# Ordering one-hots in batches of eight columns, a 52 + 28 + 80 scatter, and a three-pass mish

## Time and profile before

| | us |
|---|---|
| median of 3 runs | 2331.24 |
| lowest and highest | 2323.88, 2334.01 |
| the profiled execution's own time | 2325.94 |
| its span | 2324.2 |

### The profile page before, as it was taken

The page is one execution under the profiler, slowest core; times in us unless marked ns, Lnnn a source line. Parts: engine busy times, 40 slices in busy tenths (PEclk is TensorE's granted clock), DMA queues, the critical chain, the costliest instruction groups (busy, mean ns, idle before and its releaser), DMA issues. The chain is left out here.

```text
span 2324.2 us, 36961 instructions
## 1 busy us (share of the span) xinstructions
PE 2038.3 (88%) x11455; PEld 1106.1 (48%) x11455; DVE 1774.2 (76%) x3095; ACT 1456.0 (63%) x2429; POOL 1291.8 (56%) x1065
## 2 busy tenths in 40 slices
PE   0787688789988949999999987999999999999865
PEld 0433577546655624444444453455555554555422
DVE  8999899853333348888888853999999999999723
ACT  1999777421122225555555534999999999999822
POOL 0576677518810034444444204788888888888530
PEclk9999999989989969999999999999999999999988
DMA  2410100112143244333333304232222222222000
GB/s 114 165 27 14 55 0 0 59 32 78 41 123 98 83 139 142 93 100 99 95 93 95 71 16 134 87 92 76 77 74 76 75 74 74 77 70 78 10 0 22
DMA packets 81562, 170.33 MB, mean 73 GB/s; under 512 B 17378, under 2 KB 43221, under 8 KB 80449
## 3 DMA queue, kind: packets, MB, share of 16 engines
q0 software_dynamic: 35840, 98.88, 15.6%
q1 hardware_dynamic: 45624, 70.25, 9.1%
HBM read 144.93 MB, written 23.98 MB: 73 GB/s over the span
## 5 line engine op out<-in xcount | busy, mean ns | idle before, releaser
L884 PE MATMUL e_two_ps<-w,e_first 128*128 128x512 bf16 x1408 | 419.8, 380 | 0.1
L1629 ACT ACTIVATE u_msg<-u_t,slot_record 128x128 f32<-128x128 f32 x704 | 223.3, 390 | 98.0 <-DVE u_t L1685 97.9
L643 POOL DMA_INDIRECT sorted_records<-edge_record,slot_row x160 | 209.9, 1312 | 123.6 <-issue 57.8
L884 PE MATMUL e_two_ps<-w,e_first_low 128*128 128x512 bf16 x704 | 267.3, 380 | 0.0
L1813 POOL TENSOR_TENSOR e_first_low<-e_first 128x1024 bf16<-128x1024 f32 x88 | 250.1, 2842 | 21.9 <-DVE e_first L2004 21.9
L1818 POOL TENSOR_TENSOR e_msg_low<-e_act 128x1024 bf16<-128x1024 f32 x88 | 225.6, 2563 | 55.9 <-DVE e_act L2016 54.7
L1547 POOL DMA_INDIRECT u_got<-up_table,u_idx x176 | 185.0, 1051 | 76.8 <-issue 43.7
L2309 POOL DMA_INDIRECT e_got<-src_table,e_idx x176 | 186.6, 1060 | 70.5 <-issue 35.5
L884 PEld LDWEIGHTS e_two_ps<-w,e_first 128*128 128x128 bf16 x1408 | 134.4, 98 | 148.6 <-issue 2.2
L685 PE MATMUL pairs_ps<-cell_high,src_hot 128*128 128x144 bf16 x1180 | 153.0, 227 | 44.5 <-POOL cell_rest L709 22.4
L1593 PE MATMUL u_sum_ps<-u_msg,u_hot 128*125 128x512 f32 x352 | 185.1, 608 | 7.5 <-ACT u_msg L1629 7.5
(11 more groups left out here) (366 smaller groups left out, 5140.6 us busy)
## 6 DMA issues: line engine op xcount, KB each, us to landing
conv_w<-in_L_gnn_basis_dram SPq DMA_DIRECT2D x8, 1024.0 KB
sorted_records<-pairs SPq DMA_DIRECT2D x5, 1408.0 KB, 10.9
edge_record<-in_edge_floats_dram SPq DMA_DIRECT2D x2, 3125.0 KB
later_w<-in_L_gnn_W_dram SPq DMA_DIRECT2D x6, 1024.0 KB
attr_parts<-h SPq DMA_DIRECT2D x22, 256.0 KB, 2.1
e_attrT<-attr_parts SPq DMA_DIRECT2D x44, 128.0 KB
e_dst_all<-dst_row SPq DMA_DIRECT2D x44, 125.0 KB
pairs<-in_edge_floats_dram SPq DMA_DIRECT2D x1, 3125.0 KB
```

Of the source, the lines that this page charges most:

```text
L643: pg.nc.gpsimd.indirect_dma_start(out=pg.sorted, out_offset=bass.IndirectOffsetOnAxis(ap=pg.slot_row[:, j:j + 1], axis=0), in_=pg.edge_rec ...
L884: last = nc.tensor.matmul(out, lhsT, rhs, start=(n == 0), stop=(n == len(pairs) - 1))
L1629: last = nc.scalar.activation(msg[:, k, at * MUL:(at + 1) * MUL], t12[:, k % 2, of], ACT.Copy, scale=pg.record[:, bass.ds(t, 1), Y + m])
```

## The change: what it does

1. **Ordering.** The loop goes over 20 batches of eight columns. For each, DVE runs four TENSOR_TENSOR operations on 16-bit operands: the lane one-hots (1024 elements per partition), the tile one-hots (1888), the key parts (2048) and all three weight parts (3072). Arrays are laid out with the eight columns innermost, so each matmul reads both of its operands with a step of eight elements (16 bytes). There are two buffers rather than four. PE's products stay 40 per batch. A constant `iota_eights` of 1888 elements is added. ACT makes no weight parts; it clears `pairs` in 16 pieces of 690 floats. POOL clears 12,800 floats ahead of its scatters and the last 4,960 (which hold one-hots in the loop) after `placed`. The semaphore `decoded` goes.
2. **Scatter.** 52 columns in `order_pairs`, 5 + 23 in `layer0` around the bias additions, 80 in the first convolution as before. The late records come in two DMAs: 52 columns in `build_pairs`, 28 at the end of SP's work in `layer0`, once all 80 have landed; ACT's last work in `layer0` waits for the second and names their ends.
3. **Mish.** Exp; DVE makes `(e + 2) * e` where it clamped; Ln with a scale and a bias; Exp. The Square passes go.
4. **Destination rows.** PE reads the table of destination rows directly, at an index that its own queue loads in each `first_layer`; the copy L1974 and DVE's register load go.
5. **One-hots of the edge MLP.** `e_hotT` and `e_hot` are made by one TENSOR_TENSOR each; POOL makes `lane_rows` once.
6. `place_edges`: one more ACT copy, and six copies of the ends rather than four.

The second copies of functions that differ only in a number (mish 2, for one) are left out of the diff.

```diff
+FIRST = 52
+BATCH = 8
...
+LOG_SCALE = 0.75 * 2.0 ** -64
+LOG_BIAS = 2.0 * LOG_SCALE
+SHARE_BIAS = float(np.log(2.0) + np.log(LOG_SCALE))
...
+    pg.iota_eights = pg.hT[:, :, :].rearrange("p f n -> p (f n)")[:, PT:PT + PT * BATCH // 2].bitcast(BF16)\
+        .rearrange("p (t j) -> p t j", j=BATCH)
...
+            nc.gpsimd.iota(pg.iota_eights[:, :, :], [[1, PT], [0, BATCH]], base=0, channel_multiplier=0,
+                           allow_small_or_imprecise_dtypes=True)
...
+            act.wait_ge(sem["weight_left"], 2)
+            nc.scalar.copy(weight_16[:, 2, :], pg.weight_part[:, 2, :])
+            for ends, at in ((pg.edge_record[0:EP, 0:EARLY, SRC:SRC + 2], slice(0, EARLY)),
+                             (pg.late_ends, slice(EARLY, EARLY + FIRST)), (pg.last_ends, slice(EARLY + FIRST, EC))):
...
+        lane_hot = pg.sb("pair_lane_hot", [EP, 2, P, BATCH], BF16, ctx)
+        BATCHES, WAITED = EC // BATCH, 4
+        CLEARED = (EC - EARLY) * RECORD + EC * BUCKETS
+        pairs = pg.pairs[:, :, :, :].rearrange("p s n d -> p (s n d)")
+        HOTS = pairs.shape[1] - (3 * P + PT) * BATCH
+        weight_hot = pairs[0:EP, HOTS:HOTS + 3 * P * BATCH].bitcast(BF16).rearrange("p (s c l j) -> p s c l j", s=2, c=3, l=P)
+        tile_hot = pairs[0:EP, HOTS + 3 * P * BATCH:].bitcast(BF16).rearrange("p (s t j) -> p s t j", s=2, j=BATCH)
...
+        key_hot = room[0:EP, 0:2 * P * BATCH].bitcast(FP16).rearrange("p (s c l j) -> p s c l j", s=2, c=2, l=P)
...
             nc.gpsimd.memset(zero[:, :], 0.0).then_inc(zeroed, 1)
+            nc.gpsimd.memset(pairs[:, 0:CLEARED], 0.0)
             pool.wait_ge(pg.emptied, 16 * 5)
-            scatter_records(pg, range(0, EARLY))
-            pool.wait_ge(decoded, 1)
-            pairs = pg.pairs[:, :, :, :].rearrange("p s n d -> p (s n d)")
-            size = pairs.shape[1] // 4
-            for n in range(1, 4):
-                nc.gpsimd.memset(pairs[:, n * size:(n + 1) * size], 0.0)
+            scatter_records(pg, range(0, FIRST))
+            pool.wait_ge(placed, 1)
+            nc.gpsimd.memset(pairs[:, HOTS:], 0.0)
...
+            for i in range(BATCHES):
+                s = i % 2
+                pe.wait_ge(keys_hot, i + 1)
+                for j in range(BATCH):
                     for c in range(2):
-                        nc.tensor.matmul(column(c), key_hot[:, s, c, :], tile_hot[:, s, :], start=False, stop=False)
-                    pe.wait_ge(weights_hot, STRIDE * i + n + 1)
+                        nc.tensor.matmul(column(c), key_hot[:, s, c, :, j], tile_hot[:, s, :, j], start=False, stop=False)
+                pe.wait_ge(weights_hot, i + 1)
+                for j in range(BATCH):
                     for c in range(3):
-                        last = nc.tensor.matmul(column(2 + c), weight_hot[:, s, c, :], tile_hot[:, s, :],
+                        last = nc.tensor.matmul(column(2 + c), weight_hot[:, s, c, :, j], tile_hot[:, s, :, j],
                                                 start=False, stop=False)
-                    last.then_inc(free, 1)
+                last.then_inc(free, 1)
...
+            size = (HOTS - CLEARED) // (BATCHES - WAITED)
+            for i in range(BATCHES):
+                act.wait_ge(lanes_hot, i + 1)
+                if i >= WAITED:
+                    act.wait_ge(pg.emptied, 16 * 5)
+                    at = CLEARED + (i - WAITED) * size
+                    to = pairs[:, at:at + size]
+                    nc.scalar.activation(to, pg.ones[:, 0:1].broadcast_to(list(to.shape)), ACT.Copy, scale=0.0)
...
+            def over(x, size):
+                return x.rearrange("p (a j) -> p a j", a=1).broadcast_to([EP, size, BATCH])
+            def parts(x):
+                return x.rearrange("p c (a j) -> p c a j", a=1).broadcast_to([EP, x.shape[1], P, BATCH])
+            def lanes(s, size):
+                return lane_hot[:, s, :, :].rearrange("p (a l) j -> p a l j", a=1).broadcast_to([EP, size, P, BATCH])
+            for i in range(BATCHES):
+                s = i % 2
+                at = slice(BATCH * i, BATCH * (i + 1))
+                dve.wait_ge(free, i + 1)
+                nc.vector.tensor_tensor(lane_hot[:, s, :, :], pg.iota_eights[0:EP, 0:P, :], over(pg.pair_lane[:, at], P),
+                                        ALU.is_equal).then_inc(lanes_hot, 1)
+                nc.vector.tensor_tensor(tile_hot[:, s, :, :], pg.iota_eights[0:EP, :, :], over(pg.pair_tile[:, at], PT),
+                                        ALU.is_equal)
+                dve.wait_ge(lanes_hot, i + 1)
+                nc.vector.tensor_tensor(key_hot[:, s, :, :, :], lanes(s, 2), parts(pg.key_part[:, :, at]),
+                                        ALU.mult).then_inc(keys_hot, 1)
+                nc.vector.tensor_tensor(weight_hot[:, s, :, :, :], lanes(s, 3), parts(pg.weight_16[:, :, at]),
+                                        ALU.mult).then_inc(weights_hot, 1)
...
-            dve.sem_inc(decoded, 1)
...
+def late_records(pg, sp, begin, end):
+    sp.dma_start(pg.edge_record[0:EP, begin:end, :],
+                 pg.inp["edge_floats"].rearrange("(p j) r -> p j r", j=EC)[:, EARLY + begin:EARLY + end, :])\
+        .then_inc(pg.record_in, 16)
+def name_ends(pg, begin, ends):
+    for n, column in enumerate((SRC, DST)):
+        pg.nc.scalar.copy(pg.edge_record[0:EP, begin:begin + ends.shape[1], column], ends[:, :, n])
...
+            sp.wait_ge(pg.scattered, 16 * FIRST)
+            late_records(pg, sp, 0, FIRST)
...
+            name_ends(pg, 0, pg.late_ends)
...
             load_conv_weight(pg, conv, sp, 0)
+            sp.wait_ge(pg.scattered, 16 * EARLY)
+            late_records(pg, sp, FIRST, EARLY)
...
+            act.wait_ge(pg.record_in, 32)
+            name_ends(pg, FIRST, pg.last_ends)
...
+            scatter_records(pg, range(FIRST, FIRST + 5))
             pool.wait_ge(bias_in, 16)
             for b in range(NB):
                 nc.gpsimd.tensor_tensor(pg.x[:, b, :], pg.x[:, b, :], bias[:, :], ALU.add).then_inc(biased, 1)
+            scatter_records(pg, range(FIRST + 5, EARLY))
...
-                pool.wait_ge(pg.record_in, 16)
+                pool.wait_ge(pg.record_in, 32)
                 scatter_records(pg, range(EARLY, EC))
...
+                at = nc.tensor.value_load(pg.block_of_group[0:1, bass.ds(g, 1)], min_val=0, max_val=NB - 1)
                 pe.wait_ge(mish1_ready, n + 1)
                 if u == 0:
                     pe.wait_ge(hotT_ready, g + 3)
-                    pe.wait_ge(dst_ready, g + 1)
...
-                    nc.tensor.matmul(ps, dst_part[:, h, 0, cols], hotT[:, h, :], start=True, stop=False)
-                    nc.tensor.matmul(ps, dst_part[:, h, 1, cols], hotT[:, h, :], start=False, stop=False)
+                    for part in range(2):
+                        rows = by_dst[:, bass.ds(at, 1), part, cols].rearrange("p b d -> p (b d)")
+                        nc.tensor.matmul(ps, rows, hotT[:, h, :], start=(part == 0), stop=False)
...
-            def square1(n, u):
-                act.wait_ge(clamped1, n + 1)
-                nc.scalar.activation(act1[:, u, :, :], act1[:, u, :, :], ACT.Square,
-                                     bias=pg.ones[:, 0:1]).then_inc(act1_chain, 1)
...
+                act.wait_ge(widened1, n + 1)
+                nc.scalar.activation(act1[:, u, :, :], act1[:, u, :, :], ACT.Ln, scale=LOG_SCALE,
+                                     bias=pg.log_bias[:, 0:1]).then_inc(logged1, 1)
...
+                act.wait_ge(logged1, n + 1)
                 nc.scalar.activation(act1[:, u, :, :], act1[:, u, :, :], ACT.Exp, scale=-1.0,
-                                     bias=pg.ln2[:, 0:1]).then_inc(den1_ready, 1)
+                                     bias=pg.share_bias[:, 0:1]).then_inc(den1_ready, 1)
...
-                square2(n, u)
                 log2(n, u)
                 if more:
-                    square1(n + AHEAD, u)
+                    log1(n + AHEAD, u)
                 share2(n, u)
-                if more:
-                    log1(n + AHEAD, u)
...
-                nc.vector.tensor_copy(dst_part[:, h, :, :].rearrange("p a d -> p (a d)"),
-                                      by_dst[:, bass.ds(at, 1), :, :].rearrange("p b a d -> p (b a d)"))\
-                    .then_inc(dst_ready, 1)
...
-                nc.vector.tensor_scalar(hotT[:, h, :], dst_all[:, h, :], pg.lane_no[0:BN, 0:1], None,
+                nc.vector.tensor_tensor(hotT[:, h, :], dst_all[:, h, :], gathers.lane_rows[:, :],
...
-                for k in range(TG):
-                    last = nc.vector.tensor_scalar(hot[:, h * TG + k, :], pg.iota16[:, :],
-                                                   pg.dst_in_block[:, bass.ds(g * TG + k, 1)], None, ALU.is_equal)
-                last.then_inc(hot_ready, 1)
-            def clamp1(n, u):
+                nc.vector.tensor_tensor(
+                    hot[:, h * TG:(h + 1) * TG, :],
```

(66 more changed lines are left out.)

84 lines of the change are left out of this document (31 added, 53 removed).

## The result

The changed kernel took 2552.41 us (median of 4 runs, 2546.49 to 2553.61) against 2331.21: a ratio of 1.0956, 95% interval 1.0938 to 1.0974. It is 221 us slower where 33 us less had been forecast. The profiled execution took 2546.49 us, its span is 2544.6.

The account below looks back on a forecast made before the run. One-hot making on DVE and ACT bounds the ordering loop, PE `layer0` and the edge MLP. Terms +2 - 40 - 2 + 16 - 8 = -32 on 2325.9 profiled (2331.21 median) gave 2298 us; range 2266 to 2334.

Parts of the forecast that it names:

- The ordering loop: Ordering stage: fewer, larger DVE operations on batches of eight bring the loop from 144.4 to 104 us, -40.
- PE's 4.3 is hidden by DVE's 4.66, narrowly: Ordering loop, per batch: 40 products at 0.107 us stay below DVE's 4.66 us, so DVE binds.
- rival B: Ordering loop: products reading operands 16 bytes apart make PE the bound; at twice 0.107 us 2370; chance in full 0.05.
- DVE's price: Ordering loop: DVE's four operations at 0.54 ns per element plus overhead, 4.66 us a batch, 93 us for 20.
- The +8 us of stretch: Ordering loop: DVE operations stretched beside the scatters, perhaps 80 of them at 0.1 us on average, +8.
- Rival D: Ordering loop: one-hots made at one element per cycle, 1.07 ns, +45 for -40, 2384 in all; chance 0.04.
- Decoding: Decoding stage: POOL's clearing no longer beside DVE's L626 gives -2.4; with scatters reaching in, -3 to +4, taken as -2.
- The bound of 190 us: POOL in the ordering: 52 scatters reach 156, or 190 at worst if DVE's two-input operations hold them.
- `layer0`: `layer0`: 28 added scatters, their landing, the DMA and ACT's naming lengthen the stage by +8 to +22, taken as +16.
- Edge MLP: Edge MLP: three ACT passes instead of four shorten its start, end and PE's idle time in the middle, sum -8.
- The size of the start: Edge MLP's start: three to five shorter passes come off PE's 11.7 idle us, -3.5 to -5.9.
- Constants: Constants stage: POOL's iota of 1888 elements at 1.06 ns each, 2.0 us on the engine that ends it, +2.

Follow-up runs that it names:

- e1: The changed kernel with the ordering products reading the tile one-hots (moving operand) as dense rows, sums left wrong: 2305.8 us, loop 93.2.
- e2: The changed kernel with key and weight one-hots (stationary operand) read densely, tile one-hots still 16 bytes apart, sums left wrong: 2547.6 us, loop 337.6.
- e5: The changed kernel with tile one-hots made dense, one TENSOR_SCALAR per column; only weight loads read 16 bytes apart: 2321.96 us, ratio to before 0.9969.
- e3: The changed kernel with batches of four edge columns, both operands read 8 bytes apart: 2373.7 us, loop 172.1.
- e4: The changed kernel with batches of two edge columns, both operands read 4 bytes apart: 2368.6 us, loop 108.2, decoding 86.0.
- e9: e5 with tile one-hots from one TENSOR_TENSOR in column pairs, read 4 bytes apart, and GpSimd naming late ends in the first convolution: 2293.47 us.
- e10: The kernel before with the three-pass mish alone: 2324.96 us, stretch from the edge MLP's first one-hot to the end 899.9.
- e11: The kernel before with only PE reading destination rows directly, with its own register load per first layer: 2329.2 us, same stretch to the end 910.6.
- e8: e4 with VectorE waiting at the end of each batch for its own last operation: 2325.2 us, loop 120.8, decoding 32.5.

## Why the prediction was wrong

**The ordering loop (-40, measured +197.7).** The step that failed is "PE's 4.3 is hidden by DVE's 4.66, narrowly": it took 0.107 us for each product from rows in which the operand lies dense. The mechanism was in the text as rival B, with its point of decision at 0.117 us, and given 5% at full size because nothing in the rows spoke for it or against it. Both its chance and its size were off: it was priced at twice, 2370, and was four times, 0.428 us. The unknown cost had been bounded from one side only. e1, e2 and e5 show that it lies in the moving operand; e3, e4 and e9 show that it goes with the step.

The rule cited beside B, from the Trainium skill ("SBUF — State Buffer", section "Door 1: The DMA port swizzle"), that an access which goes to a new line of 16 bytes each time pays, pointed the right way. Its form, full rate from two accesses to a line on, is not what e3 shows: at 8 bytes of step two elements share a line, and the product took 0.212 us. The eight bf16 elements that the prediction took from it as the edge of what is free cost four times. The measurement decides.

**DVE's price** was 4.46 us a batch for the 4.66 taken. The +8 us of stretch was wrong in kind: beside the scatters DVE's TENSOR_TENSORs are not stretched in e1 (those of 2048 elements take 1214 to 1234 ns); it is GpSimd that waits. Without the strided read the change is at 2306 (e1), only 8 above the forecast of 2298, and that nearness is luck. Against the profiled execution before, e1's loop gave 51 us for the 40, and this was taken back by `layer0` (+24 for +16), the decoding (+2 for -2), the edge MLP (-4 for -8) and 6 us between `layer0` and the edge MLP, in stages that e1 doesn't touch. That stretch took 919 to 926 us in the runs.

**Rival D** (1.07 ns per element) fell: 0.52 ns.

**Decoding (-2, measured +0.7).** POOL's clearing no longer stands beside L626, but its last part now stands at the start of the decoding, beside another TENSOR_SCALAR, which ends with it: 2.89 us, where it takes 0.28 in e1. That gives back the 2.4 that had been reckoned as gained.

```profile
410.67 4.23 POOL L480 MEMSET pairs<- 128x4960 f32 x1 [241.48 <-PE pair_slots_ps L505]
412.15 2.89 DVE L595 TENSOR_SCALAR h<-h 128x236 int32<-128x236 f32 x1
```

**GpSimd in the ordering.** The bound of 190 us for the end of the scatters was met by e1, whose last one ended at 191. In the changed kernel the long waits of DVE left them free: the last one ended at 169.2.

**`layer0` (+16, measured +24.0).** The mechanism was right, and what was mis-sized is the chain of scatters: it ended 71.2 us behind the stage's start, where 54 to 67 had been reckoned. The five scatters ahead of the bias additions took 644.5 to 655.8, 11.3 us for the 7.5 (each of the first three over 2.3 for 1.19); the additions started 3.7 us later for it, but were shorter, so that they ended 1.4 us later. The 23 behind them took 49.9 us, where 34.3 to 47 had been reckoned. The prediction counted three L964 beside them. All four (L996 in the changed kernel) held one, 3.3 to 3.7 us each, and so did the TENSOR_TENSOR that splits the weights of the layer (2.1 us). What follows came as reckoned: DMA and its start 10.6 us, from SP's issue at 714.0 to ACT's start, for 10.8.

**Edge MLP (-8, measured -4.1).** The size of the start was right, but partly by luck: GpSimd's ninth `e_msg_low` comes 5.7 us earlier in the changed kernel (107.5 for 113.2 us after the first `e_hotT`), but the mish alone gives 3.3 of it (e10). The distance from Exp to Exp fell by a whole pass only once, from 5.7 to 4.6; the next two are 5.7 for 5.9, since ACT then waits for PE or DVE. The first Exp itself stands 5.0 us behind the first `e_hotT` for 6.9, and 4.8 in e11: the direct rows alone give that, which the prediction had put at nothing. The last `e_msg_low` is 7.6 us earlier. Of that 3.5 is given back behind it, in PE's products of the node MLP, which nothing in the change touches. Groups of the changed kernel, then of e10 (before: 649 ns):

```profile
L916 PE MATMUL tail_out<-later_w,u_nodesT 128*125 128x512 f32 x40 | 24.5, 771 | 4.1 <-DVE u_nodesT L2572 4.1
```

```profile
L890 PE MATMUL tail_out<-later_w,u_nodesT 128*125 128x512 f32 x40 | 21.8, 696 | 4.1 <-DVE u_nodesT L2555 4.1
```

The mean granted clock of the last 50 us was 0.74 in the changed kernel, 0.81 in e10 and 0.83 before, after a stretch of 50 us in which PE was busy for 42.0, 40.6 and 40.6 us:

```profile
2494.60:2544.60 50.00, 24.19 (x52) 10.25 (x52) 19.09 (x38) 11.02 (x16) 0.00 (x0) 0.74 0.08 26
```

So in this execution the end of the kernel took part of the gain back through PE's clock. It need not belong to the change: e3, with the same edge MLP, had 0.84 and 649 ns there (39.4 us busy in the 50 before), and its stretch from the first `e_hotT` to the end was 896.0 us. Why the clock is lower in some of the kernels was not tried.

**Constants (+2, measured +3.2).** GpSimd's iota of 1888 elements, with each value repeated eight times, took 3.46 us, 1.8 ns per element, against 1.06 for the one of 640:

```profile
1.39 3.46 POOL L139 IOTA hT<- 128x1888 bf16 x1
```

## What to carry to other kernels

A layout that lets VectorE work in fewer and longer operations changes how TensorE reads the result; price that read first, and where no row shows its step, measure one product at that step before anything is summed. Give the innermost dimension just the width that the producer needs for its fast rate and the moving operand can bear, here two 16-bit elements, and put the rest of the batch outside. Where GpSimd has descriptors to write, expect VectorE's operations with two inputs to hold it up, and leave it pauses.

## What the runs showed of the hardware

- The moving operand in bf16, 236 columns at the upper clock: 0.103 (e5) to 0.107 us dense, 0.110 at a step of 4 bytes (e9), 0.212 at 8 (e3), 0.428 at 16 (the changed kernel). The stationary one at 16 bytes: the load takes 146 ns for 98, unseen behind the products (e1, e5).
- Sixteen-bit TENSOR_TENSORs with short dense rows of 2, 4 or 8 elements, their inputs repeated over outer dimensions, run at 0.52 ns per element (e4, e3, the changed kernel).
- VectorE's TENSOR_TENSORs of 0.28 to 0.55 us back to back can hold a GpSimd scatter up until they end: 95.4 us for one of 1.19 us in e4. A wait of VectorE for its own operation, some 0.1 us, lets them through (e8). At operations of 0.7 to 1.8 us two scatters pass in 4.46 us without such a wait (e1); why they pass there and not in e4 was not tried.
- In the other direction a TENSOR_SCALAR of 236 elements took 10.49 us beside GpSimd's clearing and ended with it (e5), and so did one in the decoding of the changed kernel (2.89 us), while TENSOR_TENSORs in the place of the first (the changed kernel, e9) were not held.
